# Attention with a relative bias and experts on one core: operand images in DRAM, one load per quarter of the bias windows, tables loaded for two heads, and two steps of the bias moved to slots 4 and 8

## What is computed

```python
idx = clip(j - i, -31, 31) + 31                      # 63 buckets
attn = einsum('bhid,bhjd->bhij', q, k)               # q already scaled
qL = einsum('bhid,hdm->bhim', q, rpe_k_table)
attn = attn + take_along_axis(qL, idx, axis=-1)      # bias from q, by distance
kL = einsum('bhjd,hdm->bhjm', k * scale, rpe_q_table)
attn = attn + swapaxes(take_along_axis(kL, idx, axis=-1), 2, 3)
attn = softmax(attn, axis=-1)
out = einsum('bhij,bhjd->bhid', attn, v) + (value bias by distance)
x = x + proj(out) + experts(xn)                      # xn: normalised x
```

## Time and profile before

| | |
|---|---|
| median of three executions | 1705.66 us |
| profiled execution, span | 1722.62 us, 1720.6 us |
| PE busy / PE weight load busy | 1439.5 us (84%) / 962.7 us (56%) |
| DVE / ACT / POOL busy | 1142.8 us (66%) / 802.8 us (47%) / 537.8 us (31%) |
| mean granted clock of PE | 0.856 of full speed |
| mean share of the 16 DMA engines in use | 52.5% by the main queue, 165 GB/s |

### The profile page before, as it was taken

How to read it: one execution, slowest core, us unless ns; L and a number is a source line. 1 busy time by engine, 2 the same in 40 slices (tenths; PEclk the granted TensorE clock), 3 DMA queues, 4 the chain that set the end, 5 groups by cost and what they waited for, 6 DMA issues and landing times.

```text
span 1720.6 us, 69484 instructions
## 1 busy us (share of the span) xinstructions
PE 1439.5 (84%) x29626; PEld 962.7 (56%) x29626; DVE 1142.8 (66%) x2468; ACT 802.8 (47%) x1408; POOL 537.8 (31%) x557
## 2 busy tenths in 40 slices
PE   3792788888888889888898888889898888888887
PEld 1341355555555566555567555555565555555565
DVE  7782667777777677677644666665765766665672
ACT  1341245555555455444531545554554555454554
POOL 3462111222222222212333333333333433332333
PEclk9995578888998888888965988886987998888999
DMA  3553656665565555455544656665655665556552
GB/s 86 146 165 121 188 164 187 192 192 177 172 189 172 179 166 169 150 178 159 183 147 116 206 158 175 173 175 169 181 172 148 191 179 169 158 166 173 168 135 87
DMA packets 271582, 283.20 MB, mean 165 GB/s; under 512 B 55033, under 2 KB 205682, under 8 KB 271456
## 3 DMA queue, kind: packets, MB, share of 16 engines
q1 hardware_dynamic: 259984, 274.86, 52.5%
q0 software_dynamic: 11472, 6.83, 2.8%
HBM read 171.49 MB, written 112.36 MB: 165 GB/s over the span
## 4 chain that ended last, share of the span: by engine, by line
PE 50%; DMA 17%; DVE 12%; issue 9%; POOL 5%; SPq 4%; ACT 2%; DVEq 1%; another core or an unknown queue 0%; POOLq 0%; ACTq 0%
PE PS L721 43%; DMA dq_s<-dq_d 9%; DMA dq_d<-dq_e 7%; DVE tops L1505 6%; PE PS L992 5%; POOL ajp L681 3%; DVE dq_s L1546 2%; POOL ajp L679 2%; SPq L424 1%; SPq L478 1%; ACT PT L1190 1%; SPq L545 1%; PE PS L977 1%; PE PS L953 1%; ACT dq_e L1209 0%
## 5 line engine op out<-in xcount | busy, mean ns | idle before, releaser
L1505 DVE TRANSPOSE_TENSOR_REDUCE tops<-PS 128x16 f32<-128x512 f32 x1024 | 697.1, 701 | 377.2 <-PE PS L721 349.7
L1190 ACT ACTIVATE PT<-PS 128x512 f32<-128x512 f32 x1024 | 591.8, 596 | 569.2 <-PE PS L721 561.2
L721 PE MATMUL PS<-Q,K 73*32 73x512 bf16 (+28 forms) x11904 | 714.3, 348 | 140.8 <-issue 83.1
L721 PEld LDWEIGHTS PS<-Q,K 73*32 73x32 bf16 (+1 forms) x11904 | 322.1, 105 | 357.3 <-issue 171.1
L662 POOL COPY WP<-PT 128x768 f32<-128x768 f32 x128 | 105.3, 822 | 954.9 <-PE PS L721 940.8
L721 PE MATMUL PS<-PT,Vst 128*9 128x256 f32 (+7 forms) x7552 | 361.0, 308 | 2.6 <-issue 1.9
L721 PE MATMUL PS<-WT,eye 96*32 96x96 bf16 (+2 forms) x4352 | 294.8, 218 | 1.5 <-issue 1.3
L721 PEld LDWEIGHTS PS<-PT,Vst 128*9 128x9 f32 x7552 | 192.5, 98 | 84.9 <-issue 20.9
L721 PEld LDWEIGHTS PS<-WT,eye 96*32 96x32 bf16 x4352 | 185.8, 106 | 28.7 <-issue 3.2
L992 PE MATMUL PS<-ident,dq_s 127*128 127x127 f32 x512 | 108.6, 351 | 64.4 <-DMA dq_s<-dq_d 61.5
L681 POOL TENSOR_TENSOR ajp<-dq_s,ajp 128x508 bf16<-128x508 f32 x128 | 147.6, 1153 | 10.5
(11 more groups left out here) (207 smaller groups left out, 1051.8 us busy)
## 6 DMA issues: line engine op xcount, KB each, us to landing
aj_d<-ajp SPq DMA_DIRECT2D x64, 768.0 KB
WT<-aj_d SPq DMA_DIRECT2D x768, 64.0 KB, 2.0
dq_d<-dq_e SPq DMA_DIRECT2D x64, 512.0 KB
dq_s<-dq_d SPq DMA_DIRECT2D x64, 512.0 KB
TOE<-toe_d SPq DMA_DIRECT2D x33, 768.0 KB
Q<-q_stack SPq DMA_DIRECT2D x128, 96.0 KB
K<-k_stack SPq DMA_DIRECT2D x128, 96.0 KB
q_stack<-PT SPq DMA_DIRECT2D x24, 256.0 KB, 2.5
```

The source lines that it names most:

```text
L721: return pe.matmul(o, l, r, start=start, stop=stop, skip_group_check=True)
L1190: act.activation(PT[:, TILE + N * J + 512 * half:TILE + N * J + 512 * half + 512], PS[:, 2 + u % 2, :], ACT.Exp).then_inc(s2_read, 1)
L1505: dve.tensor_reduce(tops[:, (h + 1) % 2, s // 2, 16 * (s % 2):16 * (s % 2) + 16], PS[:, s % 2, :].rearrange("p (c i) -> p c i", i=TILE), A ...
```

## The change

- The operand rows of a head stand in DRAM as one image of 60 rows (`q_img`, `k_img`), constant rows included; `load_rows` is two transfers per pass instead of five. In the opening stage each group's stores become 16 transfers instead of 10, and 4 + 5 + 8 transfers of constants stand ahead of them instead of 2: `aj_d` is set to zero (2.43 MB) and the rows of ones are written (1.57 MB).
- `aj_d` has another layout: the three bfloat16 parts of a quarter are read by one transfer of 96 partitions (`load_windows`), not three of 32. The store of `ajp` is three transfers, one per part, whose DRAM side is 4 x 32 rows of 1024 elements.
- The tables `tabq`, `tabk` are loaded for every second head.
- The distance products move from slot 11 to slot 4, their transposes from slot 5 to slot 8 (ACT's and DVE's parts with them), the transposes of the outputs from slot 9 to slot 11. `dq_d` has two buffers.
- On SP, the store of `dq_d` moves from the end of the iteration to its middle, and the load of `dq_s` from the beginning of the next iteration to the end of this one, right behind the stores of `aj_d`.

SP, one iteration in the first half of the heads, before. L545 is the store of `aj_d`, L565 that of `dq_d`, L499 the load of `dq_s`.

The diff, cut to its core (`after.py` moves the line numbers by some 20):

```diff
-ROW_M = 64
-ROW_L = 73
+ROW_M = 8
+ROW_S = 11
+ROW_L = 65
 ROW_K = 73
-ROWS = 79
-FAR = ROWS - ROW_M
+ROWS = 71
+IMAGE = ROWS - ROW_S
...
+PITCH = 1024 + TILE
...
-        q_stack = dram("q_stack", [H * HD, COMBOS, T], BF16)
-        k_stack = dram("k_stack", [H * HD, COMBOS, T], BF16)
-        q_far = dram("q_far", [H, 6, T], BF16)
-        k_far = dram("k_far", [H, 6, T], BF16)
+        q_img = dram("q_img", [H, IMAGE, T], BF16)
+        k_img = dram("k_img", [H, IMAGE, T], BF16)
...
-        dq_d = dram("dq_d", [P, DROW])
+        dq_d = dram("dq_d", [2, P, DROW])
...
-        aj_d = dram("aj_d", [3, 3, P, N], BF16)
+        aj_d = dram("aj_d", [3, 4 * WIN * PITCH], BF16)
...
+        ROWS_IN = 16 * 2
+        TABLES = 16 * 3
+        WINDOWS = 16
+        AJ_OUT = 16 * 3
+        STORES = 16 * (2 * COMBOS + 4)
+        ZEROS = 16 * (4 + 5)
...
+            def rows_out_of(img, tok, src, part, sem_):
+
+                for n in range(COMBOS):
+                    sp.dma_start(img[:, 0:COMBOS * HD, tok].rearrange("h (d n) t -> h d n t", n=COMBOS)[:, :, n, :],
+                                 src[:, part[n], :]).then_inc(sem_, 16)
...
-            sp.dma_start(dq_d[:, 0:64], Z[:, 0:64]).then_inc(zeros_out, 16)
-            sp.dma_start(dq_d[:, 64 + N:DROW], Z[:, 0:DROW - 64 - N]).then_inc(zeros_out, 16)
+            for k in range(2):
+                sp.dma_start(dq_d[k, :, 0:64], Z[:, 0:64]).then_inc(zeros_out, 16)
+                sp.dma_start(dq_d[k, :, 64 + N:DROW], Z[:, 0:DROW - 64 - N]).then_inc(zeros_out, 16)
+            each = 3 * 4 * WIN * PITCH // P
+            for at in range(0, each, 2 * N):
+                n = min(2 * N, each - at)
+                sp.dma_start(rows(aj_d, at, [[each, P], [1, n]]), Z[:, :].bitcast(BF16)[:, 0:n]).then_inc(zeros_out, 16)
+            sp.wait_ge(zcol_set, 1)
+            sp.wait_ge(pads_set, 2)
+            for half in range(2):
+                tok = slice(half * (T // 2), (half + 1) * (T // 2))
+                ones = Q2[0:H, :, :].rearrange("p a n -> p (a n)").unsqueeze(1).broadcast_to([H, 3, 2 * N])
+                for img, row in ((q_img, 48), (q_img, 57), (k_img, 51), (k_img, 54)):
+                    sp.dma_start(img[:, row:row + 3, tok], ones).then_inc(ones_out, 16)
...
-                parts_out(q_stack[:, :, tok], QP[p], Q_PART, stacks_out[p])
+                rows_out_of(q_img, tok, QP[p], Q_PART, stacks_out[p])
...
-                parts_out(k_stack[:, :, tok], KP[p], K_PART, stacks_out[p])
+                rows_out_of(k_img, tok, KP[p], K_PART, stacks_out[p])
                 sp.wait_ge(c_cut, g + 1)
                 for m in range(2):
-                    sp.dma_start(q_far[:, 3 * m:3 * m + 3, tok], CP[p][16 * m:16 * m + 16, :, :]).then_inc(stacks_out[p], 16)
-                    sp.dma_start(k_far[:, 3 * m:3 * m + 3, tok], CP[p][32 + 16 * m:48 + 16 * m, :, :]).then_inc(stacks_out[p], 16)
+                    sp.dma_start(q_img[:, 51 + 3 * m:54 + 3 * m, tok], CP[p][16 * m:16 * m + 16, :, :]).then_inc(stacks_out[p], 16)
+                    sp.dma_start(k_img[:, 48 + 9 * m:51 + 9 * m, tok], CP[p][32 + 16 * m:48 + 16 * m, :, :]).then_inc(stacks_out[p], 16)
...
-                sp.dma_start(Qx[0:48, r, :], q_stack[hh * HD:hh * HD + HD, :, tok].rearrange("d n t -> (d n) t")).then_inc(rows_in, 16)
-                sp.dma_start(Kx[0:48, r, :], k_stack[hh * HD:hh * HD + HD, :, tok].rearrange("d n t -> (d n) t")).then_inc(rows_in, 16)
-                sp.dma_start(Qx[ROW_M + 6:ROW_M + 12, r, :], q_far[hh, :, tok]).then_inc(rows_in, 16)
-                for m, row in ((0, ROW_M + 3), (1, ROW_M + 12)):
-                    sp.dma_start(Kx[row:row + 3, r, :], k_far[hh, 3 * m:3 * m + 3, tok]).then_inc(rows_in, 16)
+                sp.dma_start(Qx[ROW_S:ROWS, r, :], q_img[hh, :, tok]).then_inc(rows_in, 16)
+                sp.dma_start(Kx[ROW_S:ROWS, r, :], k_img[hh, :, tok]).then_inc(rows_in, 16)
...
-                sp.dma_start(Qd[0:48, :], q_stack[hh * HD:hh * HD + HD, :, tok].rearrange("d n t -> (d n) t")).then_inc(qd_in, 16)
-                sp.dma_start(tabq[0:48, :], tab_stack[hh * HD:hh * HD + HD, :, 0, :].rearrange("d n p -> (d n) p")).then_inc(qd_in, 16)
+                wait(sp, dq_psum, h)
+                sp.dma_start(Qd[0:48, :], q_img[hh, 0:48, tok]).then_inc(qd_in, 16)
+                if h % 2 == 0:
+                    sp.dma_start(tabq[0:48, :], tab_stack[hh * HD:hh * HD + HD, :, 0, :].rearrange("d n p -> (d n) p")).then_inc(qd_in, 16)
 
             def load_aj(h):
                 b, hh = place(h)
                 tok = slice(b * N, b * N + N)
-                sp.dma_start(Ka[0:48, :], k_stack[hh * HD:hh * HD + HD, :, tok].rearrange("d n t -> (d n) t")).then_inc(ka_in, 16)
-                sp.dma_start(tabk[0:48, :], tab_stack[hh * HD:hh * HD + HD, :, 1, :].rearrange("d n p -> (d n) p")).then_inc(ka_in, 16)
+                wait(sp, aj_psum, 2 * h)
+                sp.dma_start(Ka[0:48, :], k_img[hh, 0:48, tok]).then_inc(ka_in, 16)
+                if h % 2 == 0:
+                    sp.dma_start(tabk[0:48, :], tab_stack[hh * HD:hh * HD + HD, :, 1, :].rearrange("d n p -> (d n) p")).then_inc(ka_in, 16)
+
+            def load_distances(h):
+
+                sp.wait_ge(dq_out, 16 * (h + 1))
+                wait(sp, aj_parts, 2 * h)
+                sp.dma_start(dq_s[:, :], rows(dq_d, (h % 2) * P * DROW + 1, [[DROW + 1, P], [1, N]])).then_inc(dq_in, 16)
...
-                sp.wait_ge(aj_out, 16 * (t + 1))
+                sp.wait_ge(aj_out, AJ_OUT * (t + 1))
...
-                for part in range(3):
-                    sp.dma_start(WTb[TILE * part:TILE * part + TILE, t % PAIR, :, 2 * q:2 * q + 2, :].rearrange("p s j n -> p s (j n)"),
-                                 shear(t % 3, part, 2 * q, 2)).then_inc(wt_in[q], 16)
+                shear = rows(aj_d, (t % 3) * 4 * WIN * PITCH + TILE - 1 + 2 * P * q, [[PITCH - 1, WIN], [WIN * PITCH, 4], [1, 2 * P]])
+                sp.dma_start(WTb[0:WIN, t % PAIR, :, 2 * q:2 * q + 2, :].rearrange("p s j n -> p s (j n)"), shear).then_inc(wt_in[q], 16)
...
-            def shear(p, part, J, n):
-
-                return rows(aj_d, (3 * p + part) * P * N + TILE - 1 + P * J, [[N - 1, TILE], [TILE * N, 4], [1, P * n]])
...
-                if on(3):
-                    sp.wait_ge(dq_out, 16 * (h + 4))
-                    wait(sp, aj_parts, 2 * h + 6)
-                    sp.dma_start(dq_s[:, :], rows(dq_d, 1, [[DROW + 1, P], [1, N]])).then_inc(dq_in, 16)
-                if on(4):
-                    wait(sp, dq_psum, h + 4)
-                    load_dq(h + 4)
+                if h == hm:
+                    load_distances(h + 3)
                 load_windows(h + 1, 2)
...
+                if on(4):
+                    sp.wait_ge(dq_copied, h + 5)
+                    wait(sp, aj_psum, 2 * (h + 3))
+                    sp.dma_start(dq_d[h % 2, :, 64:64 + N], dq_e[:, :]).then_inc(dq_out, 16)
                 load_windows(h + 1, 3)
-                if on(4):
-                    wait(sp, aj_psum, 2 * (h + 4))
-                    load_aj(h + 4)
                 if on(1):
                     if h >= 0:
                         sp.wait_ge(s2_ready, SLOTS * h + 1)
                     load_rows(h + 1, Q2, K2, rows2_in)
+                if on(5):
+                    load_dq(h + 5)
+                if on(4) and h + 4 > 0:
+                    load_aj(h + 4)
+                load_windows(h + 2, 0)
...
-                load_windows(h + 2, 0)
...
-                    sp.dma_start(aj_d[t % 3].rearrange("n p x -> p n x"), ajp[:, :, :, :].rearrange("p n j d -> p n (j d)")).then_inc(aj_out, 16)
+                    for part in range(3):
+                        sp.dma_start(rows(aj_d, (t % 3) * 4 * WIN * PITCH + part * TILE * (PITCH - 1), [[WIN * PITCH, 4], [PITCH, TILE], [1, N]]),
+                                     ajp[:, part, :, :].rearrange("p j d -> p (j d)")).then_inc(aj_out, 16)
+                if on(4) and h != hm - 1:
+                    load_distances(h + 4)
...
-                if on(4):
-                    sp.wait_ge(dq_copied, h + 5)
-                    wait(sp, aj_psum, 2 * (h + 4))
-                    sp.dma_start(dq_d[:, 64:64 + N], dq_e[:, :]).then_inc(dq_out, 16)
                 load_windows(h + 2, 1)
 
+            load_dq(0)
+            load_aj(0)
...
-                    if s == 11 and on(4):
-
-                        own(qd_in, TABLES * (h + 5), TABLES)
-                        fin_free(h - 1)
...
+                    if s == 4 and on(4):
+
+                        own(qd_in, TABLES * ((h + 4) // 2) + (TABLES if h % 2 else 32), TABLES // 2)
...
-                    if s == 9 and on(-2):
+                    if s == 11 and on(-2):
...
-                    if s == 5 and on(3):
-
-                        top_free(h + 1)
+                    if s == 8 and on(3):
...
                         own(dq_in, 16 * (h + 4), 16)
-                        own(ka_in, TABLES * (h + 4), TABLES)
```

(12 more changed lines are left out.)

58 lines of the change are left out of this document (30 added, 28 removed).

## The result

The changed kernel takes 2247.7 us (median of 4 runs, 2243.9 to 2249.6) against 1713.8 for the kernel before on the same chip: ratio 1.322, 95% interval 1.314 to 1.331. It is 534 us slower. Ratios and their intervals here compare only executions in the faster of two states that this kernel's executions fall into. The forecast was 1980 us, 274 above the 1705.66 us of before, nearly all of it from one cause; the cause is there, but the time lies 138 us above the upper end of the range.

A forecast was written before the change was run, and what follows sets the result against it. PE's matmuls and the dq_d store with its dq_s reload were taken to bound the kernel. 1720.6 + 258 (slot 4 loop) + 6 (pipeline filling) + 11 (opening) = 1996 us, less 17 to the median: about 1980, range 1690 to 2110.

The forecast's parts named there:

- Direction and mechanism: Slower: ajp stores on four engines delay the window quarter, so PE waits some 5 us in slot 4; chance 0.75.
- the sum of the loop: Slot 8 transposes through stores and quarter to slot 4 and back: 26.2 us per head against 22.5, 26.8 with clock loss.
- The clock: Lower PE clock behind the slot 4 wait: 0.6 us per head added, none at the least, 1.7 at most.
- The landing: From issue of the ajp stores to the quarter's landing: 1.8 us fixed time plus 10.3 us data.
- The rest of the loop: Slot 8 transposes to issue of the stores, 8.0 us, and slot 4 to slot 8, 6.1 us.
- The opening: Before the first head: 15 more transfers ahead of the first group's stores cost 11 us, between 6.5 and 12.8.
- while the pipeline filled: First three heads pass one by one, store to transposes 11.6 us instead of 9.6: 6 us in all.
- The gain: Moved steps end PE's waits for dq_s and clock falls behind them: 67 us, not added to the sum.
- A: Rival: ajp stores spread over 16 engines, no wait in slot 4, dq_s waits go: 1648 us; chance 0.13.
- B: Rival: stores spread, but a faster iteration makes its own new wait and the start loses 11 us: 1690 us; chance 0.07.
- C: Rival: four engines at the contended rate, stores take 14.7 us instead of 8.4: 2360 us; chance 0.05.

The follow-up runs named there:

- The two shapes in the kernel before: Kernel before, store of ajp cut into three transfers: flat 128 x 1024, 1705.1 us; with a gap of 64 elements behind every 32 rows, 2159.2 us.
- spread stores: Changed kernel with the store of ajp as four transfers of 32 partitions x 3 x 1024 instead of three of 4 x 32 rows: 1919.5 us.
- the order half: Changed kernel's slots, SP order, two dq_d buffers and tables per two heads, with the old layout and its one store: 1736.5 us, 1.011 of the kernel before.
- the layout alone: Kernel before with row images, one transfer per window quarter, four-strip stores and opening constants, in old order and slots: 1841.6 us, ratio 1.069.

## Why the prediction was right or wrong

**Direction and mechanism: right.** The stores of 4 x 32 x 1024 run on four engines (DMA share 0.26). The wait is PE's for `WT<-aj_d` in slot 4, 4.9 us on average where "some 5 us" stood, and there is none for `dq_s` in the steady state. Traffic falls to 129 GB/s ("about 145"). The two shapes in the kernel before show the cause by themselves. The account of the miss: from the first head to the last it is 1966.9 us for 1481.9, 485 more where 258 stood, and the first head comes 39 us later where 17 stood.

**The step that failed: the sum of the loop, in two of its terms.** Both were too small, by 2 to 3 us per head each.

*The clock: "I add 0.6 per head for that (none at the least; at the most 3.4 us at half clock per head, 1.7)".* It came from one 3.4-us stretch behind a short wait. Measured, the clock in the heads fell from 0.88 to 0.71. With 57 rows more and the same stores it came back to 0.88, and the heads from 30.2 to 27.5 us: 2.7 us per head, above even the 1.7 at the most. Two things are in it. The wait lowers the clock by itself: the gap in the stores of the kernel before, with its matmuls as they were, added 131 us to PE's busy time in the 56 heads. And the matmuls had 8 rows less, an edit that the prediction didn't price at all: it has no term for `ROWS` going from 79 to 71. With spread stores these 8 rows are worth 67 us. Between the changed kernel and the one before, PE's busy time differs by 240 us; how these divide between wait and rows, with the stores as they are and 8 rows put back, wasn't tried.

*The landing: "a transfer's fixed time" 1.8 and "data" 10.3, together 12.1.* From the first store to the landing of the quarter it took 1529.85 - 1514.85 = 15.0 us in the round shown, and 14.4 with the 57 rows. The rate was right: 96 / 4 = 24 GB/s per engine, by which 768 KB take 8.2 us (8.4 forecast). But the stores' data flow from about 1516 to 1527, 11 us: between 1516.5 and 1518 only 8 to 41 GB/s move, while the three stores and the reload are being issued, and from 1519.5 to 1522 the other engines move data at 213 to 422 GB/s beside them. Which of the two costs the 3 us stays open. The issues themselves take longer than the 0.38 us put down, 0.56 to 1.12 each; but with spread stores the quarter is also issued 2.9 us behind the first store (3.5 here), so that is not the whole of it.

*The rest of the loop.* Transposes to store take 8.5 us (8.0 forecast) at a clock of 0.50, and slot 4 to 8 takes 7.4 to 7.65 (6.1 forecast) at 0.52. With the 57 rows, at clocks of 1.00 and 0.68, they take 7.0 and 5.9, so these excesses belong to the clock. The round shown sums to 8.5 + 15.0 + 7.4 = 30.9 us, against 26.2.

**The opening: too small.** The first head comes at 235.5 instead of 196.7, 39 us later; 11 + 6 were forecast. The timeline of SP shows the terms:

```profile
31.47 22.23 SPq L431 DMA_DIRECT2D dq_d<-PT  x1
...
55.98 4.25 SPq L436 DMA_DIRECT2D aj_d<-PT  x5
60.33 2.06 SPq L443 DMA_DIRECT2D q_img<-Q  x2
62.43 3.28 SPq L443 DMA_DIRECT2D k_img<-Q  x2
65.75 3.80 SPq L443 DMA_DIRECT2D q_img<-Q  x2
69.59 3.80 SPq L443 DMA_DIRECT2D k_img<-Q  x2
```

No issue but the first few came at the 0.43 us put down. The zeros' five take 4.25 us, 0.85 each, and the eight of the ones 13 us, 1.6 each; so the group stores behind them begin at 73.4, 19 us later than before. The first group's own 16 take 12.7 us where 10 took 6.8, and "of which little shows" was wrong: ACT waits 34.29 us for them, 25 more than before. The remaining 14 us came while the pipeline filled, where 6 were forecast.

**The gain: wrong.** 67 us were put down for the moved steps, though not added to the sum, since they lie inside the loop. Alone, the order half is 1.1% slower. The wait for `dq_s` went as forecast, and waits for window quarters (29.4 us) and for the rows of maxima (19.3 us) took its place. With more rows it is the same: 1652.0 us for 1632.0.

**Rivals.** A needed the store under 4.7 us of data; it took 8 or more. Neither its result (1648) nor B's (1690) would have come with 16 engines: the changed kernel with spread stores is at 1919.5, because both leave out the clock and most of the opening. C's rate of 13.4 GB/s per engine didn't come; 24 did. The measured time lies between the forecast and C's 2360, but for other reasons than C's.

## What to carry to other kernels

Before a store is reshaped, write down the outermost count of both its sides, with rows that follow each other without a gap counted as one run. A count of 4 on the DRAM side left a store on four engines here, and cutting a transfer of 127 rows in two freed the queue behind it; what is issued behind such transfers waits. A matmul's row count is not free even where its duration doesn't depend on it: here fillers of zeros in 49 unused rows, with two small repairs of transfers, made the kernel 5% faster, and taking 8 such rows away helped to make another slower. When a wait in a loop of TensorE is priced, look at how much lower the clock is in the slots behind it, and price these too.

## What was not expected of the hardware

- TensorE's granted clock rose with the rows of its matmuls at equal instructions, columns and transfers: over 27 heads of the layout alone 0.82 with 71 and 65 rows, 0.95 with 128 and 122, and 0.88 against 0.96 in the kernel before with 32 more; the contents of the fillers (ones or zeros) changed nothing. The Trainium skill ("TensorE: Matmul & The Clock Gate", section "What's actually happening") has the clock follow how busy TensorE has been; here it was busy for no larger share of the time (485 of 571 us with the 32 rows, 531 of 609 without), and the rows still told. Which of the matmuls counts, whether the place of the rows has a part in it, and why, stays open: the fillers widened the scores' operands and those of the distance products together.
- A transfer of 127 rows held SP's queue as well: the next issue took 22.3 us behind it, and 0.57 us once it was cut into 112 and 15.
- A long wait costs more than itself: with the same matmuls, 268 us more of idle time in 56 heads came with 131 us more of busy time, by a lower clock.
- A gap of 64 elements between blocks of 32 rows, with not a byte more to move, took a store's outermost count from 128 to 4 and the kernel from 1705 to 2159 us.
